# Indexed transfers on GpSimd issued without waits between them, and other sequence groups in the second expert layer

## The reference: what is computed

```python
x = x + 0.5 * ffn(layernorm(x))
x = x + attn(layernorm(x))         # 16 heads of 16, position bias, 8 heads forward, 8 backward
x = x + 0.5 * ffn(layernorm(x))

def ffn(x):                        # flat: 8192 tokens
    out = shared_experts(flat)     # 2 shared experts, each 256 -> 128 -> 256, for every token
    probs = softmax(flat @ router_w)
    weights, indices = top_k(probs, 2)          # 2 of 16 routed experts
    weights = weights / (weights.sum(-1) + 1e-9)
    return out + sum over the 2 chosen experts of weight * expert(flat)   # 256 -> 64 -> 256
```

## Time and profile before

| what | value |
|---|---|
| time, median of 3 runs | 2264.89 us (2262.14 to 2269.9) |
| the profiled execution's own time | 2255.13 us |
| its span, first to last instruction | 2253.3 us |
| PE busy | 1702.2 us (76%) |
| DVE busy | 1474.2 us (65%) |
| ACT busy | 1046.5 us (46%) |
| POOL busy | 947.3 us (42%) |
| mean granted TensorE clock | 0.887 |

### The profile page before, as it was taken

How to read it: one execution, slowest core, us unless ns; L and a number is a source line. 1 busy time by engine, 2 the same in 40 slices (tenths; PEclk the granted TensorE clock), 3 DMA queues, 4 the chain that set the end, 5 groups by cost and what they waited for, 6 DMA issues and landing times.

```text
span 2253.3 us, 35352 instructions
## 1 busy us (share of the span) xinstructions
PE 1702.2 (76%) x10696; PEld 1121.1 (50%) x10696; DVE 1474.2 (65%) x3920; ACT 1046.5 (46%) x2263; POOL 947.3 (42%) x999
## 2 busy tenths in 40 slices
PE   3758875678788888886877889888887677985382
PEld 2646655446455555543544546555554334553251
DVE  4765666677766657676677776766787757573432
ACT  3325543354455555554454555645554335553151
POOL 2643337454423231445444343443545635234604
PEclk8979996789999999988998989999998789997686
DMA  7468753645867666555449765666746686864895
GB/s 206 139 205 248 251 182 97 121 90 154 227 180 211 187 193 172 151 96 124 92 75 239 182 171 146 178 167 138 176 105 132 207 247 164 244 188 149 265 310 162
DMA packets 327979, 392.80 MB, mean 174 GB/s; under 512 B 40296, under 2 KB 269032, under 8 KB 327784
## 3 DMA queue, kind: packets, MB, share of 16 engines
q1 hardware_dynamic: 269520, 284.59, 48.4%
q0 software_dynamic: 24576, 67.14, 10.5%
q10 hardware_dynamic: 33696, 38.81, 5.2%
HBM read 188.58 MB, written 155.19 MB: 153 GB/s over the span
## 4 chain that ended last, share of the span: by engine, by line
PE 29%; DMA 26%; DVE 17%; issue 10%; POOL 10%; SPq 4%; ACT 3%; another core or an unknown queue 0%; ACTq 0%; DVEq 0%; POOLq 0%
DMA sorted_x<-xn,position 7%; DMA y_tok<-sorted_y,position 6%; DMA den<-o_store 4%; PE bank L1202 3%; PE bank L1098 3%; PE bank L991 3%; PE bank L1109 3%; PE bank L993 3%; PE bank L992 3%; PE bank L1182 2%; POOL sorted_x L1737 2%; DMA q_stack<-shift_t 2%; DVE x_att L1646 2%; PE bank L1215 2%; POOL y_tok L1763 2%
## 5 line engine op out<-in xcount | busy, mean ns | idle before, releaser
L1343 ACT ACTIVATE p_buf<-bank 128x512 f32<-128x512 f32 x640 | 361.8, 599 | 264.4 <-PE bank L1182 212.1
L1574 DVE TENSOR_REDUCE row_max<-bank 128x1 f32<-128x512 f32 (+2 forms) x768 | 349.2, 504 | 76.4 <-PE bank L1165 70.6
L1737 POOL DMA_INDIRECT sorted_x<-xn,position x224 | 221.4, 988 | 232.6 <-DMA sorted_x<-xn,position 140.4
L1797 POOL TENSOR_SCALAR_AFFINE_SELECT p_buf<-p_buf 128x512 f32<-128x512 f32 x256 | 161.6, 645 | 316.5 <-ACT p_buf L1343 314.9
L1182 PE MATMUL bank<-q_stack,k_stack 101*128 101x512 bf16 (+3 forms) x1024 | 244.7, 318 | 57.2 <-DMA q_stack<-shift_t 46.6
L1149 PE MATMUL bank<-k_stack,q_stack 99*128 99x512 bf16 (+3 forms) x1024 | 254.2, 319 | 32.4 <-issue 19.6
L1763 POOL DMA_INDIRECT y_tok<-sorted_y,position x192 | 185.5, 966 | 213.2 <-DMA y_tok<-sorted_y,position 117.0
L1202 PE MATMUL bank<-p_buf,v_rows 128*32 128x512 f32 (+3 forms) x2048 | 197.5, 485 | 91.0 <-POOL p_buf L1797 88.0
L1309 ACT ACTIVATE t_y<-bank 128x256 f32<-128x256 f32 x406 | 133.3, 380 | 156.4 <-PE bank L1109 137.4
L991 PE MATMUL bank<-w_down,hs_buf 128*128 128x256 f32 x256 | 89.1, 348 | 126.5 <-POOL hs_buf L1770 125.4
L1676 DVE RECIPROCAL den<-den 128x128 f32<-128x128 f32 x128 | 110.0, 913 | 101.2 <-DMA den<-o_store 99.8
(11 more groups left out here) (193 smaller groups left out, 3910.7 us busy)
## 6 DMA issues: line engine op xcount, KB each, us to landing
t_w<-expert_w SPq DMA_DIRECT2D x137, 256.0 KB
t_x<-sorted_x SPq DMA_DIRECT2D x137, 256.0 KB
sorted_y<-t_y SPq DMA_DIRECT2D x137, 256.0 KB
q_stack<-qk_part SPq DMA_DIRECT2D x192, 128.0 KB
k_stack<-qk_part SPq DMA_DIRECT2D x192, 128.0 KB
sorted_x<-zeros SPq DMA_DIRECT2D x69, 256.0 KB, 3.6
p_buf<-expert_w SPq DMA_DIRECT2D x66, 256.0 KB
p_buf<-sorted_x SPq DMA_DIRECT2D x66, 256.0 KB
```

Source lines behind the costliest of these rows:

```text
L1343: act.activation(p_of(u), psum("score", *of)[:, :], ACT.Exp).then_inc(*exp_done.step(*of))
L1574: ins = dve.tensor_reduce(row_max[g % 2][:, n:n + 1], src[:, col:col + q1 - q0], X, ALU.max)
L1737: pool.indirect_dma_start(sorted_x[l, group_of(l, b)], bass.IndirectOffsetOnAxis(ap=position[:, b, k, t:t + 1], axis=0), xn[buffer][:, t, ...
L1797: pool.affine_select(blocks, blocks, [[0, GH], [1 if ahead else -1, P]], ALU.is_ge, zero, base=0, channel_multiplier=-1 if ahead else 1).t ...
```

## The change

Two things change. First, the waits between the single transfers go: each buffer has one semaphore for all its transfers, and those who need the data wait for the full count of the last one (`2 * NT - 1`), which all eight transfers together reach. Second, the second layer's groups become sequences 0 to 7, 8 to 13, 14 and 15 (47, 39 and 23 tiles); the sum of tiles stays 109. The planner makes a new order from these groups.

```diff
-GROUPS = (((0, 6), (6, 16)), ((0, 7), (7, 13), (13, 16)))
+GROUPS = (((0, 6), (6, 16)), ((0, 8), (8, 14), (14, 16)))
...
-        sent = [[signal(f"sent{i}{n}", 16) for n in range(3)] for i in range(6)]
+        sent = [signal(f"sent{i}", 16) for i in range(6)]
...
-        gathered = [[signal(f"gathered{i}{n}", 16) for n in range(3)] for i in range(5)]
+        gathered = [signal(f"gathered{i}", 16) for i in range(5)]
...
-            i, d = norm_buffer("ffn", l, b), apart_out(l, b)
-            return [sent[i][n % d].at(l, b, n) for n in range(2 * NT - d, 2 * NT)]
...
+            return sent[norm_buffer("ffn", l, b)].at(l, b, 2 * NT - 1)
...
-                    if n >= apart_out(l, b):
-
-                        pool.wait_ge(*sent[buffer][n % apart_out(l, b)].at(l, b, n - apart_out(l, b)))
...
-                        xn[buffer][:, t, :], None).then_inc(*sent[buffer][n % apart_out(l, b)].step(*of))
+                        xn[buffer][:, t, :], None).then_inc(*sent[buffer].step(*of))
...
-                    y, landed = tail_y[y_buffer(l, b)], gathered[y_buffer(l, b)][n % apart_back(l, b)]
-                    if n >= apart_back(l, b):
-
-                        pool.wait_ge(*landed.at(l, b, n - apart_back(l, b)))
+                    y, landed = tail_y[y_buffer(l, b)], gathered[y_buffer(l, b)]
```

More of the change, by code:

```diff
@@ L704, in build @@
         out_put = [signal(f"out_put{i}", 16) for i in range(2)]
-        sent = [[signal(f"sent{i}{n}", 16) for n in range(3)] for i in range(6)]
+        sent = [signal(f"sent{i}", 16) for i in range(6)]
         filled, filled_act = signal("filled", 16), signal("filled_act", 16)
-        gathered = [[signal(f"gathered{i}{n}", 16) for n in range(3)] for i in range(5)]
+        gathered = [signal(f"gathered{i}", 16) for i in range(5)]
         def all_sent(l, b):
-            i, d = norm_buffer("ffn", l, b), apart_out(l, b)
-            return [sent[i][n % d].at(l, b, n) for n in range(2 * NT - d, 2 * NT)]
-        def all_gathered(l, b):
-            i, d = y_buffer(l, b), apart_back(l, b)
-            return [gathered[i][n % d].at(l, b, n) for n in range(2 * NT - d, 2 * NT)]
+            return sent[norm_buffer("ffn", l, b)].at(l, b, 2 * NT - 1)
         tx_in = [signal(f"tx_in{i}", 16) for i in range(7)]
@@ L853, in do @@
                         sp.wait_ge(*x_put[0, b].at(b))
-                        for landed in all_sent(0, b):
-                            sp.wait_ge(*landed)
+                        sp.wait_ge(*all_sent(0, b))
                         for d in range(ND):
@@ L878, in do @@
                         for b in sent_all(l, g):
-                            for landed in all_sent(l, b):
-                                sp.wait_ge(*landed)
+                            sp.wait_ge(*all_sent(l, b))
                     if before["t_x", l, g, j]:
@@ L1272, in do @@
                         if old_kind == "ffn":
-                            for landed in all_sent(old_l, old):
-                                act.wait_ge(*landed)
+                            act.wait_ge(*all_sent(old_l, old))
                     for t in range(NT):
@@ L1546, in find @@
                 dve.wait_ge(*place_step.at(*newest["placed"], "position"))
-                for landed in all_sent(l, b):
-                    dve.wait_ge(*landed)
+                dve.wait_ge(*all_sent(l, b))
                 dve.wait_ge(*table_step.at(l, g, "row"))
@@ L1638, in do @@
                     dve.wait_ge(*x_got[l, b % (3 - l)].at(b))
-                    for landed in all_gathered(l, b):
-                        dve.wait_ge(*landed)
+                    dve.wait_ge(*gathered[y_buffer(l, b)].at(l, b, 2 * NT - 1))
                     dve.wait_ge(*route_step.at(l, b, "share"))
```

## The result

The changed kernel takes 2232.28 us (median of 4 runs, 2229.85 to 2234.91) against 2263.51 for the kernel before in the same comparison (4 runs, 2259.68 to 2269.9): a ratio of 0.9859, 95% interval 0.9832 to 0.9887, or 31 us faster. The forecast was 2135; of the 130 us it promised, a quarter came. The profiled execution's own time is 2229.85, its span 2228.0.

What follows compares the result with a forecast made beforehand. No engine was full for long; engines in fixed orders waited for each other, partly for POOL's landings. 22 + 60 + 20 + 20 + 18 - 10 = 130 us off 2255.1 gave 2125, plus 9.8 to the median: 2135 us, range 2060 to 2235.

Steps and rivals of the forecast that it cites:

- they stay hidden, with some 20 us of cover; beyond it each fetch costs its 1.25 us: At the end, the second group's 48 fetches need 60 us, covered by about 81 us before the last tile's landing.
- The first rival: The waits between transfers only change place, so only the groups count, 38 us: 2227 us; chance 0.17.
- First stages, 22 us: From 165 to 425, half of POOL's 45.5 us of waits for landings goes: 22 us off, bounds 0 and 45.5.
- Attention, 60 us: From 425 to 1704, 60 us off, a little under the 68 us of PE's late start behind POOL; bounds 0 and 152.
- the prediction's last sentence: The 60 us in attention is trusted least: waits tell only what came last, POOL or ACT's exponentials just ahead.
- First group's stage, 20 us: From 1704 to 2052, 20 of POOL's 52 us of waits go, while its wait for `combine` grows; bounds 0 and 52.
- The groups, 20 us ahead of the last scores: Ten tiles fewer on PE before the last scores (72 for 82): 20 us off, bounds 0 and 26.
- The end, 18 us: After the last scores, 27 us saved by scatter, tiles and last fetches, 9 us charged for moved tiles; bounds -10 and 27.
- Contention, 10 us on `den`: In attention, batches of eight on busy DMA engines lengthen DVE's 78.4 us of waits for `den` and its like: 10 us lost.
- the rival of bursts that hold up attention's transfers: In attention each of 32 `den` transfers lands later; at 6 us later the kernel is 52 us slower, 2317; chance 0.07.
- The Trainium skill's rule on a transfer's length: For POOL's 128 KB transfers, an estimated 2.3 us each; then removed waits were empty and the groups alone counted.

Runs made afterwards that it cites:

- e1: The changed kernel (no waits between transfers) with the groups of before (0 to 6, 7 to 12, 13 to 15): 2202.7 us, ratio 0.9758 to the kernel before.
- e5: e1 with 24 fetches added that POOL issues in a row beside the last group's 27 tiles: 2232.0 us, ratio 0.9877 to the kernel before.
- e6: e5 with each of the 24 added fetches waiting for the landing three before: 2212.2 us, ratio 0.977 to the kernel before.
- e2: The kernel before, with its waits kept, given the new groups: 2282.2 us, ratio 1.0082 to the kernel before.
- e3: The changed kernel with a wait for the landing three transfers earlier on the 48 fetches of sequences 8 to 13 alone: 2198.9 us, ratio 0.9736.
- e11: The changed kernel with 0.65 us of other POOL work ahead of each of the 48 fetches, no waits for landings: 2207.6 us, ratio 0.9749.

## Why the prediction was wrong

The sign was right, and so was the mechanism of the waits: they were not empty, and PE waited less for POOL without them. Two steps failed. The larger is the end: "they stay hidden, with some 20 us of cover; beyond it each fetch costs its 1.25 us". It costed the 48 fetches by POOL's time and by the landing at their end, as if only their own length could matter. Their cost was to the tiles beside them: 123 us for 23 tiles. The end was forecast 18 us shorter and is 43 longer, 61 us off. The second is attention: the 60 us were taken from the 68 by which PE's waits behind POOL would fall. These waits fell by 85 us, and the stage by 7 (28 in e1), as other waits stood close behind. Between the two profiled executions 25 us came of the 130, so the forecast missed by 105 (by the medians 97): 61 at the end, 53 in attention and 13 ahead of it, less 12 that the stage after it gave beyond its 40 and the 10 that the forecast had kept for contention.

The first rival's 2227 us lies 5 us from the measured time, and that is luck: it held that the waits were worth nothing and the groups 38 us, and the runs show 55 to 60 us for the waits and a loss for the groups.

Step by step:

- *First stages, 22 us:* e1's first scores come at 409 for 425, 16 us earlier, the changed kernel's 9, and e5's, with e1's order and without waits as well, only 1 (424). So the gain is below the forecast, and single executions do not tell its size.
- *Attention, 60 us:* mis-sized, as said. From the first scores to those of sequence 13 it took 1279 us before, and 1251 in e1, whose order is the same (1253 and 1264 in e5 and e6). PE's waits behind POOL fell by more than the 68 us on which I built: in e1's stretch (409 to 1660), of 106 us, 19 are left (L1196), beside waits that have nothing to do with POOL:

```profile
PE bank L1176 <- DMA q_stack<-shift_t: 39.0, 17, 8.1
PE bank L1103 <- DVE t_h L1624: 34.0, 17, 5.6
...
PE bank L1196 <- POOL p_buf L1782: 19.3, 20, 2.5
```

  PE's idle time, though, fell only by 37 us, from 1279 - 1054 = 225 to 1251 - 1063 = 188: other waits took over, PE's wait for DVE's part of a tile (L1103) from 18 to 34 us among them. A wait's length in the view is what came last, not what would be won, as the prediction's last sentence allowed for.
- *First group's stage, 20 us:* 347 us before, 327 in e1. Right, and POOL's wait for `combine` grew from 25 to 29 us there, as forecast.
- *The groups, 20 us ahead of the last scores:* not there with the old waits. From the first to the last scores e2 took 1645 us, for 1626 before, with PE busy 1323 and 1327 us: ten tiles fewer, but at a mean granted clock of 0.89 for 0.91. Without waits, the changed kernel's 1567 and e1's 1578 leave 11 us. That is about the spread of executions: the others with the order of e1 (e5, e6) took 1579 and 1591, those with the changed kernel's order and its free transfers up to there (e3, e11) 1565 and 1573.
- *The end, 18 us:* the parts that I listed came: the scatter of sequence 15 in 10 us (2045 to 2055), the last fetches in 21 for 31, and the scatter 62 us after the last scores for 54, 8 us where I charged 9. The sum took 8.5 us off for four tiles fewer; the 23 tiles took 45 us more than the 27 (123 for 78). The part costed at nothing was the large one.
- *Contention, 10 us on `den`:* 78 to 86 us in attention, and so about right (PE's wait for `shift_t` grew too, from 39 to 49, though not in e1); the rival of bursts that hold up attention's transfers is out in that form. Its idea, that bursts hurt others, was the right one in another place and on another path.

The Trainium skill's rule on a transfer's length (page "DMA: Bandwidth & Descriptors", section "Anatomy of one DMA"), by which, as the prediction worked it out, the removed waits were empty, is not borne out here: the waits gave 55 to 60 us.

## What to carry to other kernels

A wait that looks useless can be a throttle: before a row of transfers is set free, look for what runs beside it, and keep the pace where the row lies beside a chain of short steps between engines. When a new order puts work beside the critical chain, cost it by what that chain's engines must do in between (here six combines in DVE's order), not by whether its own length is covered. Try each part of a two-part change alone: 31 us faster was 55 to 60 won and 23 to 30 lost.

## What the runs showed of the hardware

A long row of indexed transfers on GpSimd, 1.25 us each, goes with PE's signals coming 10 to 29 us late (2080.93 to 2091.35 and 2101.21; 2082.13 to 2111.01). At 1.75 us each the same order's tiles took 98 us for 123. Bandwidth is not the limit: the DMA engines are less busy in the row than with pauses in it (80% for 95%). Nor is the number in flight: by the bytes moved it is about two fetches at either pace. Signals of ACT and DVE came within 0.1 us in the same stretch (PE at 2092.04 and 2123.74), while ACT and SP both got PE's late. What stays open is why the rate matters, and whether PE's signal is late or its result. The Trainium skill, page "Perfetto Trace Analysis", section "Tensor Engine Instruction (MATMUL, LD_WEIGHTS)", says that a matmul's end in the profile is an estimate and that its signal leaves only after the writes to PSUM have been acknowledged; the trace here fits both, as PE's end times are modelled.
